# GpSimd keeps two additions, one product and the gathers: bias, moments and dot sums go to VectorE, the LRN pixels to ScalarE, two TensorE transposes to DMA, in a new order of all queues

## The reference

```python
x = x + _L0_conv_ref(_ln_c(x), ...)      # best of 512 vectors per 3x3 patch, then a small MLP
t = t + _L0_ffn_ref(_ln_t(t), W1, b1, W2, b2)
x = x + _L1_conv_ref(_ln_c(x))           # LRN: x / (2 + 1e-4 * box5x5(sum_c x*x)) ** 0.75
t = t + _L1_ffn_ref(_ln_t(t), W1, b1, W2, b2)
```

## Time and profile before

| | |
|---|---|
| median of 3 runs | 3559.07 us |
| the profiled execution, its own time | 3554.84 us |
| its span, first to last instruction | 3553.0 us |
| busy TensorE, VectorE, ScalarE, GpSimd | 85%, 78%, 80%, 72% |
| steps between 417.50 and 3264.44 us | 2846.94 us, repeating every 206.9 us (eight steps) |
| the last 289 us | the last tiles drain: only the LRN and the feed-forward parts run |

### The profile page before, as it was taken

How to read it: one execution, slowest core, us unless ns; L and a number is a source line. 1 busy time by engine, 2 the same in 40 slices (tenths; PEclk the granted TensorE clock), 3 DMA queues, 4 the chain that set the end, 5 groups by cost and what they waited for, 6 DMA issues and landing times. The chain is left out here.

```text
span 3553.0 us, 62660 instructions
## 1 busy us (share of the span) xinstructions
PE 3011.0 (85%) x18190; PEld 1688.2 (48%) x18190; DVE 2778.1 (78%) x10043; ACT 2832.7 (80%) x7303; POOL 2566.0 (72%) x3993
## 2 busy tenths in 40 slices
PE   5888888888888888888888888888888888888755
PEld 2444454454545445445544545454444555445432
DVE  6777888888888888888888888888888888888631
ACT  0444788888888888888888888888878888888977
POOL 2455787777778777777877777787777778777753
PEclk9999999999999999999999999999999999999855
DMA  3111121211112121111212111121212112121000
GB/s 88 38 45 47 45 63 52 65 54 57 61 57 62 52 67 51 57 61 56 62 52 67 52 58 60 57 62 52 66 51 64 55 57 62 52 66 42 24 31 35
DMA packets 64607, 195.78 MB, mean 55 GB/s; under 512 B 11394, under 2 KB 14732, under 8 KB 64268
## 3 DMA queue, kind: packets, MB, share of 16 engines
q1 hardware_dynamic: 54028, 172.89, 15.1%
q0 software_dynamic: 10240, 18.89, 2.1%
HBM read 134.72 MB, written 57.02 MB: 54 GB/s over the span
## 5 line engine op out<-in xcount | busy, mean ns | idle before, releaser
L527 ACT ACTIVATE ffn_hid<-banks 128x384 f16<-128x384 f32 x2304 | 1026.8, 487 | 260.0 <-PE banks L370 236.7
L393 PE MATMUL banks<-wcT,xc 128*128 128x512 f32 x2304 | 1187.8, 618 | 50.2 <-DVE mx L745 43.4
L745 DVE TENSOR_REDUCE mx<-banks 128x1 f32<-128x512 f32 x1152 | 781.4, 687 | 428.8 <-PE banks L393 427.6
L370 PE MATMUL banks<-ffn_xT,w1q 128*128 128x384 bf16 x2304 | 668.8, 343 | 177.3 <-ACT ffn_hid L527 138.0
L994 POOL TENSOR_TENSOR ffn_f<-ffn_y,b2q 128x864 f16<-128x864 f16 x256 | 465.3, 1818 | 288.3 <-DVE nb L731 209.7
L370 PEld LDWEIGHTS banks<-ffn_xT,w1q 128*128 128x128 bf16 x2304 | 226.1, 98 | 775.8 <-ACT ffn_hid L527 589.4
L393 PEld LDWEIGHTS banks<-wcT,xc 128*128 128x128 f32 x2304 | 414.5, 196 | 282.8 <-issue 140.8
L825 DVE TENSOR_SCALAR ffn_hid<-ffn_hid,b1q 128x1152 f16<-128x1152 f16 x768 | 405.8, 551 | 139.0 <-ACT ffn_hid L527 138.6
L996 POOL TENSOR_TENSOR x<-x,ffn_f 128x864 f32<-128x864 f32 x256 | 466.6, 1823 | 20.1
L560 ACT ACTIVATE ffn_x<-x,cols 128x96 fp8e5<-128x96 f32 x1152 | 461.3, 456 | 0.0
L560 ACT ACTIVATE ffn_x<-x,nb,roots 128x96 fp8e5<-128x96 f32 x1152 | 425.1, 456 | 0.0
(11 more groups left out here) (153 smaller groups left out, 4178.6 us busy)
## 6 DMA issues: line engine op xcount, KB each, us to landing
xt<-x_tok_in SPq DMA_DIRECT2D x128, 432.0 KB, 3.2
xc<-x_chan_in SPq DMA_DIRECT2D x128, 432.0 KB, 3.6
out_tok<-x SPq DMA_DIRECT2D x128, 432.0 KB
win<-x_tok_in,xrow POOLq DMA_INDIRECT x128, 2.6
wrow<-vector_table,vidx POOLq DMA_INDIRECT x128, 2.9
shift<-shift_in SPq DMA_DIRECT2D x1, 960.0 KB
vector_table<-wtab SPq DMA_DIRECT2D x1, 384.0 KB, 2.9
w1raw<-w_in SPq DMA_DIRECT2D x1, 288.0 KB
```

The source lines that it names most:

```text
L370: last = pe.matmul(bank[:, 0:GW], w1q[:, ffn.layer, c * P:(c + 1) * P], ffn.xT[:, g * GW:(g + 1) * GW], start=True, stop=True)
L393: last = pe.matmul(ps_score[score_bank(j)], xc[p][:, j, :], wcT[:, :], start=True, stop=True)
L527: return nc.scalar.activation(dst, src, ACT.Copy)
L745: nc.vector.tensor_reduce(mx[p][:, j:j + 1], ps_score[score_bank(j)], AX.X, ALU.max).then_inc(score_taken, 1)
```

## The change

It does the following.

- **Turning by DMA.** The e5m2 pixels are written in pairs, two bytes wide (`x8` is [P, 5, P, 2]), and one DMA transpose from SyncE per ffn and step (`turn`) writes `xT`, which TensorE reads as e5m2. The three transpose units per tile and their copies on ScalarE are gone. The first product is now cut in 512, 512 and 128 columns, still nine units. `turn(ffn0)` waits for `norm0`; `turn(ffn1)` for `norm1` of the tile that the next step uses. On the SyncE queue the order is turn ffn0, store, loads, turn ffn1.
- **ScalarE** scales all nine LRN pixels (`lrn_pixels`), not five.
- **VectorE** gets both b2 additions (`ffn_bias`, fp16), the moments (seven operations, interleaved with `select`), the whole sum of the dot products over 96 channels (128x864, before 128x432), and one small operation more in `mlp_input`. The three accumulator sums of `select` become one product and one reduction over 27 columns.
- **GpSimd** keeps, in this order: the addition of ffn0, the gather of the vector's row, one copy for the image, at an image's end `window_parts` (with two more products), the product with the nine pixels, the addition of ffn1, one copy of columns, the gather of the pixel.
- **Orders.** All engines' orders are written anew.

```diff
+            def turn(ffn, tile):
+                sp.wait_ge(ffn.x8_ready, tile + 1)
+                wait_past(sp, ffn.filled, tile * UNITS - 2)
+                sp.dma_start_transpose(ffn.xT[:, :, :], ffn.x8[:].rearrange("p a c t -> p (a c t)").bitcast(F16)
+                                       ).then_inc(ffn.turned, 16)
...
+            def body(k):
+                if k.back is not None:
+                    turn(ffn0, k.back)
                 if k.rtail is not None:
                     sp.wait_ge(x4_ready, k.rtail + 1)
                     sp.dma_start(out[k.rtail], x4[k.q][:]).then_inc(x4_stored[k.q], 16)
+                load(Step(k.k + 1))
+                if k.pre is not None:
+                    turn(ffn1, k.pre)
...
+                    if u < HC * G:
+                        c, g = divmod(u, G)
...
-                            last = pe.matmul(bank[0:C, i * P:(i + 1) * P], ffn.x8[:, u * G + i, :],
-                                             ident_b[:, :], start=True, stop=True)
-                    elif u < G + HC * G:
-                        c, g = divmod(u - G, G)
-                        if c == 0:
-                            pe.wait_ge(ffn.taken, tile * UNITS + 2 + g + 1)
-                        last = pe.matmul(bank[:, 0:GW], w1q[:, ffn.layer, c * P:(c + 1) * P],
-                                         ffn.xT[:, g * GW:(g + 1) * GW], start=True, stop=True)
+                            pe.wait_ge(ffn.turned, (tile + 1) * 16)
+                        c0, c1 = COLUMNS[g]
+                        pairs = ffn.xT[:, c0 // (2 * P):(c1 + P) // (2 * P), :].bitcast(F8).rearrange(
+                            "p a (x t) -> p a t x", t=2)
+                        if g == G - 1:
+                            pairs = pairs[:, :, 0:1, :]
...
-                        last = copy(ffn.xT[0:C, u * GW:(u + 1) * GW], bank[0:C, 0:GW])
-                    elif u < G + HC * G:
-                        c, g = divmod(u - G, G)
-                        last = copy(ffn.hid[:, c, g * GW:(g + 1) * GW], bank[:, 0:GW])
...
+                    if u < HC * G:
+                        c, g = divmod(u, G)
+                        c0, c1 = COLUMNS[g]
+                        last = copy(ffn.hid[:, c, c0:c1], bank[:, 0:c1 - c0])
...
-                    last = nc.scalar.activation(ffn.x8[:, j, :], x[:, j, :], ACT.Identity, bias=bias_c[:, j:j + 1],
+                    last = nc.scalar.activation(ffn.x8[:, j // 2, 0:C, j % 2], x[:, j, :], ACT.Identity, bias=bias_c[:, j:j + 1],
...
+                take_hidden(ffn1, k.rear, 8, 1)
+                norm0(k, 7, J)
+                lrn_pixels(k, 4, XA)
+                lrn_pixels(k, XA, 6)
+                norm1(k, 0, 1)
+                lrn_pixels(k, 6, 8)
+                norm1(k, 1, 2)
+                take_hidden(ffn0, k.back, 0, 1)
+                norm1(k, 2, 3)
+                take_hidden(ffn0, k.back, 1, 2)
+                norm1(k, 3, 4)
+                lrn_pixels(k, 8, J)
+                take_hidden(ffn0, k.back, 3, 2)
+                take_out(ffn1, k.rear, k.rear_p, 0)
+                take_hidden(ffn0, k.back, 5, 1)
+                norm1(k, 4, XA)
+                take_hidden(ffn0, k.back, 6, 3)
+                norm1(k, XA, J)
+                take_out(ffn1, k.rear, k.rear_p, 1)
...
+                wait_past(dve, root_ready, tile)
+                wait_past(dve, kept, tile - 6)
+                mc.begin(tile)
+                of = lambda i: st3[:, :, :, i]
+                d, m2 = mtmp[:, 0, :, :], mtmp[:, 1, :, :]
+                mc.add(nc.vector.tensor_tensor(d, of(1), of(4), ALU.subtract),
+                       nc.vector.tensor_tensor(m2, of(2), of(5), ALU.add))
+                yield
+                mc.wait()
+                mc.add(nc.vector.tensor_tensor(d, d, d, ALU.mult))
+                yield
+                mc.add(nc.vector.tensor_tensor(twice[p], of(1), of(4), ALU.add))
+                yield
+                mc.wait()
+                mc.add(nc.vector.scalar_tensor_tensor(out=ssq[p], in0=d, scalar=C / 4.0, in1=m2, op0=ALU.mult,
+                                                      op1=ALU.add))
+                yield
+                mc.wait()
+                mc.add(nc.vector.scalar_tensor_tensor(out=args[:, 0:3, :], in0=ssq[p], scalar=1.0 / C,
+                                                      in1=eps[:, :, :], op0=ALU.mult, op1=ALU.add),
+                       nc.vector.tensor_copy(args[:, 3, :], ssq[p][:, 1, :]))
+                assert mc.done == mc.per
...
+                one = pick[p][:, :].rearrange("p (o j) -> p o j", o=1).broadcast_to([P, 3, J])
+                f1c.add(nc.vector.tensor_tensor(junk[:, :, :], pix[p][:, :, 1, :], one, ALU.mult))
+                yield
+                f1c.wait()
+                nc.vector.tensor_reduce(chosen[p][:, 0:3], junk[:, :, :], AX.X, ALU.add).then_inc(pick_ready, 1)
...
+                f3c.add(nc.vector.tensor_reduce(dots[:, :], prod_dot[:, :, :], AX.X, ALU.add),
+                        nc.vector.tensor_scalar(mix[:, 0:1], chosen[q][:, 2:3], top_q, None, ALU.mult),
+                        nc.vector.tensor_scalar(mix[:, 2:3], chosen[q][:, 0:1], 0.5, None, ALU.mult),
+                        nc.vector.tensor_scalar(mix[:, 1:2], top_q, -1.0, 1.0, ALU.mult, ALU.add))
+                meanwhile()
...
+                    b2 = b2q[:, ffn.layer, :].rearrange("p (o c) -> p o c", o=1).broadcast_to([P, J, C])
+                    nc.vector.tensor_tensor(ffn.f[:, :, :], ffn.y[:, :, :], b2, ALU.add).then_inc(ffn.f_ready, 1)
             def lrn_columns(n, pre):
...
             def body(k):
-                between = pixel_roots(k) if k.moments is not None else iter(())
-                def scores(j0, j1, links=0):
+                roots_of = pixel_roots(k) if k.moments is not None else iter(())
+                factors = lrn_columns(k.lrn, k.pre) if k.lrn is not None else iter(())
+                last = None
+                def scores(j0, j1, between=iter(()), links=0):
                     for j in range(j0, j1):
```

429 lines of the change are left out of this document (207 added, 222 removed).

## The result

The changed kernel takes **3363.43 us**, the median of 4 runs (3360.04 to 3366.41); the kernel before, on the same chip, 3559.36 (3557.28 to 3559.89). The ratio is 0.945, with a 95% interval of 0.9434 to 0.9467: 196 us faster. The profiled execution is the one of 3366.41 us, with a span of 3364.6; busy are TensorE 84%, VectorE 90%, ScalarE 78% and GpSimd 35%.

The account below looks back on a forecast made before the run. A loop of VectorE's half and TensorE's half through the convolution bounds each step: 15.17 + 8.93 + 0.1 = 24.2 us. Eight steps take 202.3, 4.6 less; 14 rounds save 64 us, giving 3495 us, range 3380 to 3665.

Parts of the forecast that it names:

- The loop: From convolution end through VectorE's work to ffn0's rounding, then TensorE's to the next convolution end: 24.87 us, bounding the step.
- VectorE alone bounds: Rival: TensorE and ScalarE hand-overs nearly vanish, the step is VectorE's 23.1 and 0.2 us; 3394 us; chance 0.14.
- my forecast: Plain step falls to 24.2 us, eight steps to 202.3, predicted time 3495 us; chance 0.43.
- VectorE's half: Convolution end to the end of ffn0's rounding: 9.99 us before, 8.93 after the change.
- the 0.3 added for the relu's wait: In VectorE's half, the last relu waits 0.3 us for ScalarE's last copy, taking 8.63 to 8.93.
- TensorE's half with its hop: From ffn0's rounding to the next convolution's end: 14.31 us before, 15.17 after, plus 0.1 for the hop to TensorE.
- I take two more of them: In TensorE's half, two added waits for hidden units' bank copies at 0.33 us each, taking 14.51 to 15.17.
- The image's end: The two steps at an image's end cost 1.7 and 7.0 us beyond plain ones, 8.7 per eight steps.
- The collision rival: GpSimd's product starts first and VectorE's rounding of ffn1 waits: 1.6 us a step in seven of eight, 3651 us; chance 0.20.
- Late turns: DMA turns take 3.6 us, not 3.0; two places each stall 0.6 us, 1.2 a step; 3629 us; chance 0.17.
- nothing waits for what is left but the gather and product below: GpSimd sheds moments, biases, half sums and LRN pixels; no other engine waits on its remaining work except gather and product.
- The clock: A sign of being wrong: granted clock under 1.00 in plain steps, which would stretch TensorE's half.

Follow-up runs that it names:

- run 6: Run 1's kernel with the sum of the dot products made twice on VectorE; 3394.52 us.
- run 12: Run 11's kernel with ScalarE's two relus to h1 moved ahead of one normalisation and one copy; 3345.65 us.
- run 13: Run 1's kernel with the last relu and the rounding of ffn0 moved ahead of the last eight small operations of select and moments; 3314.00 us.
- run 5: Run 1's kernel with the b2 addition of ffn1 left out on VectorE; 3314.74 us.
- run 10: Kernel before with turns by DMA and the change's order on TensorE and ScalarE, scores 2 and 5 in their old places, GpSimd and VectorE work unchanged; 3558.71 us.
- run 11: Run 1's kernel with score 5 behind the convolution again on TensorE, its maximum behind the residual on VectorE; 3419.54 us.
- run 1: The changed kernel, but GpSimd waits for VectorE's rounding of ffn1 before its product with the nine pixels; 3327.27 us.
- run 4: The changed kernel, GpSimd's product split and VectorE's rounding of ffn1 waiting for its first pixel and a short fill in plain steps, forcing the collision; 3486.51 us.
- run 14: Run 1's kernel with both b2 additions given back to GpSimd, each ahead of its residual addition; 3575.59 us.
- run 9: Kernel before with all nine LRN pixels on ScalarE, none on GpSimd; 3697.69 us.
- run 8: Kernel before with pixels turned by DMA and ffn0's normalisation ahead, between ScalarE's copies of ffn1; 3645.53 us.

## Why the prediction was right and wrong, step by step

**The loop was the right thing to look at.** Runs 6, 12 and 13 move the step by what they do to one of its halves, and run 5, which touches neither, leaves it. The rival "VectorE alone bounds" named 23.3 us and 3394, closer than my forecast, but not its cause: run 5 takes 0.5 us off VectorE and the plain step stays.

**VectorE's half, 8.93 predicted, 8.52 measured.** The part that failed is the 0.3 added for the relu's wait. The 14 small operations start 0.12 apart, as summed (2565.82 and 2565.94 in the timeline), but stand inside the time in which ScalarE's last copy is awaited; wait and work are one stretch, not two. Run 13 shows it from the other side.

**TensorE's half with its hop, 15.27 predicted, 14.56 measured.** The step that failed is "I take two more of them": the 0.66 us of new waits for bank copies. In the clean step two such waits are left, of 0.16 and 0.15, where one of 0.38 stood before. The rest, 14.31 + 1.88 - 1.30 - 0.38 + 0.1 = 14.61, fits to 0.05 us, but partly by luck: it left out the 0.88 us that the convolution waits for `h1` once score 5 is gone from in front of it (runs 10, 11, 12). Score 5's 0.94 us is free. I had priced a move of work on a busy engine at its duration, without asking what that engine would wait for in its absence.

**The image's end, 8.7 predicted, about 6.0 measured** (27.2 + 25.0 + 22.9 and five of 23.1 make 190.6, less eight of 23.1). Both guesses were too high. From one convolution's end to the next the step that builds the box takes 23.08, nothing more than a plain one where I had 1.7. The LRN step takes 27.1 to 29.0, so 4.0 to 5.9 more where I had 7.0; in seven of the fourteen the granted clock is 0.5 for 3.4 us. GpSimd's addition did run into the small operations, as forecast: in all fifteen LRN steps the first of them (L935) takes 1.44 us, and 0.19 at the drain.

```profile
2668.82 1.82 POOL L1080 TENSOR_TENSOR x<-x,ffn_f 128x864 f32<-128x864 f32 x1 [7.08 <-DVE nb L777]
2669.25 1.44 DVE L935 TENSOR_SCALAR lbuf<-lbuf 128x72 f32<-128x72 f32 x1
```

**The sum.** Fourteen cycles of eight steps average 194.7 us in the changed kernel and 206.7 before: 168 us of the 188 by which the profiled spans differ; start and end give the other 20, where I counted nothing. Without collisions and late turns the cycle is 190.2 (run 1's undisturbed ones are 190.0 to 190.3), 16.5 less than before, or 231 us in fourteen. Run 1's cycles average 191.8: late turns and small rest take 22 of it. The other 40 went to collisions, and 28 of them at 1.5 to 1.6 us are 42 to 45. Against the forecast of 202.3 a cycle the undisturbed 190.2 are 12.1 less, 169 us in fourteen; with the 62 for disturbances and the 20 at both ends that is 127, and the profiled execution came out 125 below its forecast (3366 against 3491).

**The collision rival (0.20) came true in part.** Its mechanism, its place and its price were right: 1.6 us a step predicted, 1.5 to 1.6 measured in VectorE's half, and it was decided within tenths, as said. It happened in 28 steps, where run 4 could force it in 86. What I did not see is that it and the late turns are not two cases: in this trace each collision came behind a late turn. Since it was added to a base that was 1.1 us too slow a step, the case gave 3651 where every plain step forced to collide takes 3486.

The Trainium skill's rule on this ("SBUF — State Buffer", SBUF: two separate sides), that whichever of the two starts first holds the ports for its whole instruction, agrees with 2.75 and 2.77 us in the two orders.

**Late turns (0.17) came true in part.** The turn lands 2.6 us after its issue, the gather's end of my two; it rises to 3.4 and more in a stretch of the run. The estimate from the Trainium skill's 1309 ns for a 128x128 block ("VectorE: DVE Perf Modes", The three transpose paths), taken five times in a row, was 6.5 us: the measurement decides against the blocks going one after the other.

**Prices.** The fp16 addition is 0.60 us, 0.5 was taken; the dot sum 1.05, so 0.46 more than before, where 0.5 was taken. These fell into TensorE's half, where run 5 shows that nothing came of one of the additions. VectorE was summed at 23.1 us busy a step and has 22.4; I did not take that apart.

**What I left out.** "GpSimd's moments, biases, half sums and LRN pixels leave it; nothing waits for what is left but the gather and product below" was costed at nothing. Run 14 shows that what GpSimd does decides when its next operation starts, and that this start is worth 1.4 to 1.6 us of VectorE's half; in run 9 the same thing happened to the rounding and cost nothing, which the trace shows and does not explain. The clock I had only as a sign of being wrong. It is 1.00 in the plain steps shown, but runs 8, 9 and 14 show what it takes where TensorE is left waiting. The gain is no sum of parts: turns alone are +85 us, LRN alone +137, turns with the order 0, all of it -196, and all of it with run 1's wait but the bias additions back on GpSimd +14.
